# Cross-attention block in split f16: TensorE's program without a loop, maxima over the partitions by TensorE and VectorE, two weight loads later, causal mask added by VectorE

## The chip, the cores and the metric

The kernel runs on 1 core of one Trainium2 chip. A core has five engines that run programs of their own and meet at semaphores: TensorE (PE, with its weight loads as PEld), VectorE (DVE), ScalarE (ACT), GpSimd (POOL) and SyncE (SP), which here issues every DMA. The metric is the device time in microseconds (us) of one execution; lower is better.

## The reference

Eight batches of 1024 queries attend to 64 context rows of their own view, with 16 heads of 32 columns, and a feed-forward layer of 2048 follows:

```python
q = _layer_norm(query, ln1_g, ln1_b)
qh = (q @ wq + bq).reshape(Bq, Sq, H, hd)
kh = (context @ wk + bk).reshape(Bq, Sc, H, hd)
vh = (context @ wv + bv).reshape(Bq, Sc, H, hd)
scores = jnp.einsum('bqhd,bkhd->bhqk', qh, kh) * scale
allowed = pos_in_block[None, :] <= jnp.arange(Sq)[:, None]
scores = jnp.where(allowed[None, None, :, :], scores, NEG_INF)
probs = jax.nn.softmax(scores, axis=-1)
o = jnp.einsum('bhqk,bkhd->bqhd', probs, vh).reshape(Bq, Sq, Dm)
x = query + (o @ wo + bo)
h = _layer_norm(x, ln2_g, ln2_b)
return x + jax.nn.gelu(h @ w1 + b1, approximate=False) @ w2 + b2
```

Query is 8 x 1024 x 512, context 8 x 64 x 512, all f32. With 64 keys the causal mask touches only the first 64 queries of a batch, so only the first tile of 128 queries.

## The kernel before, in words

**Arithmetic.** Every f32 matrix product is made of three f16 products (`triple`, L1060: high x high, high x low, low x high). The f16 parts need a power-of-two scale for each operand, found at run time from the largest magnitude of each weight, bias and context matrix. Each partition's own maximum goes into a column of `maxima`; the maximum over the 128 partitions is needed on all of them in `gmax`. There are four such rounds: 0 (context, wk, wv, bk, bv), 1 (wq, first norm, query bias), 2 (wo, second norm, w1, its bias) and 3 (w2). Before, GpSimd does a round with `partition_all_reduce` in `reduce_maxima` (L478), at four places in its program.

**Stages.** A prologue transposes the context, finds scales, projects keys and values of all batches (`values`, in part inside the first slot) and takes the query tiles 0 to 3 through the first norm. Then come 17 slots. Slot c handles the attention of chunk c (512 queries, 4 tiles of 128; an even c starts a batch) and, woven between, the feed-forward of chunk c-1. Slots 0 and 16 have one half only. A slot has 19 groups; group g issues the first feed-forward product g (L1060 into ff1_ps), the attention steps that the tables `PLAN` or `PLAN_FIRST` (slot 0) give at position 2g, the second product g-3 (L1267), and the steps at position 2g+1. Each engine walks the same table and does its share of a step.

**Steps.** Q: query projection; S: scores of a tile on TensorE (L1184), row maximum (L985) and subtraction (L987) on VectorE; E: exponential on ScalarE; U: row sum and reciprocal on VectorE; then GpSimd divides (L540, `normalise`); Z, L: split into high and low f16 (ScalarE, VectorE), after which SP issues a DMA transpose of the probabilities (L419); V: values product (L1206), which waits for all four transposes; O: output projection, residual and norm statistics; H (slot 0) or G, D: second norm; W (slot 0): values product of the context. GpSimd also makes the reciprocal deviation of every norm (`rstd_of`, L483) in program order with its other work.

**Mask.** At tile 0 of an even slot two matmuls (L1178) first write the mask, `causal`, into the score bank with the identity `ident_bf`, and the score matmuls add to it.

**Loops.** In `slots` every engine writes slots 0 and 1 out, runs slots 2i+2 and 2i+3 in a hardware loop of 7 passes (GpSimd, ScalarE, VectorE and SP of 6, with the last two slots written out) and ends with slot 16.

**Loads.** SP's program is one ordered queue: context, wk, wv, wq, the first x tiles, wo, four pieces of w1, w2 pieces 2 and 3, then `move_values` (copies inside SBUF that wait for the values), then w2 pieces 0 and 1 (their place in SBUF is taken by early data until then), then slot 0's `move_probs`. ScalarE takes the magnitudes of w2 pieces 0 and 1 (L608) at position 20 and 21 of slot 0.

## Time and profile before

| | us |
|---|---|
| median of 3 runs | 1900.4 |
| range | 1899.72 to 1901.34 |
| the profiled execution, its own time | 1901.46 |
| the span in its trace | 1899.7 |

| engine | busy us | share |
|---|---|---|
| TensorE matmul | 1801.5 | 95% |
| VectorE | 1240.3 | 65% |
| ScalarE | 628.6 | 33% |
| GpSimd | 437.3 | 23% |

A trace row gives start, duration, engine, source line, operation, output and inputs, and in brackets how long the engine was idle before it and what ended that. "issue" is time in which the engine waited for nothing that the trace shows.

### The profile page before, as it was taken

To read this page: it belongs to the slowest core of one execution; us is meant where nothing else is said; L and a number is where in the kernel's file an instruction comes from. 1 tells how busy PE (TensorE), PEld (TensorE's weight loads), DVE (VectorE), ACT (ScalarE), POOL (GpSimd) and SP (SyncE) were. 2 spreads that over 40 slices of the span, in tenths; PEclk is the share of its full clock that TensorE was granted. 3 is DMA by queue.
4 is the path that set the end of the run, shared out by engine and by line. 5 is a ranking of instruction groups with operands and counts; after the bars stand their busy time and mean duration, and the time that the engine had idled before them with its cause. 6 is when DMAs were issued, how large, how long until landed. Compare 5 with 4: busy or idle time off the path is not lost.

```text
span 1899.7 us, 26840 instructions
## 1 busy us (share of the span) xinstructions
PE 1801.5 (95%) x10214; PEld 819.9 (43%) x10214; DVE 1240.3 (65%) x1905; ACT 628.6 (33%) x786; POOL 437.3 (23%) x380
## 2 busy tenths in 40 slices
PE   4737899999999999999999999999999999999999
PEld 2313344444444444444444444444444444444444
DVE  5757966757676675757676575767667576766632
ACT  3434523333242422324242232424233242424211
POOL 2431313122131313203141211313131121313200
PEclk9868999999999999999999999999999999999999
DMA  8051230413323141322314042231404123230300
GB/s 282 12 122 34 45 89 6 84 45 56 79 45 89 23 79 35 62 72 45 90 23 89 23 79 57 45 89 33 95 8 89 45 50 85 45 90 7 60 23 22
DMA packets 287751, 116.48 MB, mean 61 GB/s; under 512 B 262616, under 2 KB 264192, under 8 KB 287616
## 3 DMA queue, kind: packets, MB, share of 16 engines
q1 hardware_dynamic: 287616, 114.61, 27.5%
q8 instruction: 93, 1.52, 0.3%
q14 instruction: 42, 0.34, 0.1%
HBM read 31.22 MB, written 16.78 MB: 25 GB/s over the span
## 4 chain that ended last, share of the span: by engine, by line
PE 89%; DVE 5%; issue 2%; DMA 1%; ACT 1%; SPq 1%; POOL 1%; DVEq 0%; POOLq 0%; ACTq 0%
PE ff_ps L1060 34%; PE ff_ps L1267 33%; PE at_ps L1060 17%; PE at_ps L1184 2%; PE at_ps L1206 1%; DVE w_all L781 1%; DMA arena<-qT 1%; SPq L419 1%; DVE ssum L1003 0%; DMA arena<-in_L_xattn_wk 0%; DVE arena L781 0%; DVE xhat L770 0%; DVE stats L748 0%; DVE arena L987 0%; DVE smax L985 0%
## 5 line engine op out<-in xcount | busy, mean ns | idle before, releaser
L1060 PE MATMUL ff_ps<-arena,w_all 128*128 128x512 f16 x3072 | 703.8, 381 | 11.2 <-ACT arena L710 5.1
L1267 PE MATMUL ff_ps<-w_all,arena 128*128 128x512 f16 x3072 | 698.0, 379 | 0.8 <-DVE arena L781 0.8
L1060 PEld LDWEIGHTS ff_ps<-arena,w_all 128*128 128x128 f16 x3072 | 300.1, 98 | 384.1 <-issue 25.2
L1267 PEld LDWEIGHTS ff_ps<-w_all,arena 128*128 128x128 f16 x3072 | 294.3, 98 | 358.5 <-issue 6.4
L710 ACT ACTIVATE arena<-ff_ps,b1p,scales 128x512 f32<-128x512 f32 x256 | 198.7, 776 | 648.6 <-PE ff_ps L1060 648.3
L1033 DVE TENSOR_SCALAR arena<-arena,scales 128x512 f16<-128x512 f32 x256 | 140.9, 551 | 220.5 <-ACT arena L710 220.5
L781 DVE SCALAR_TENSOR_TENSOR arena<-arena,scales 128x512 f16<-128x512 f32 x256 | 240.1, 938 | 9.1
L483 POOL TENSOR_TENSOR rstd<-ve,minus_half 128x1 f32<-128x1 f32 x128 | 85.8, 670 | 545.8 <-DVE ve L753 537.8
L535 POOL TENSOR_TENSOR x_sb<-x_sb,bo_row 128x512 f32<-128x512 f32 x64 | 90.8, 1450 | 353.0 <-PE at_ps L1184 353.0
L648 ACT ACTIVATE norm_hl<-xhat 128x512 f16<-128x512 f32 x120 | 73.9, 628 | 290.6 <-DVE xhat L770 290.6
L540 POOL TENSOR_TENSOR arena<-arena,rsum 128x1024 f32<-128x1024 f32 x64 | 124.8, 1971 | 180.7 <-DVE rsum L1006 180.7
L1060 PE MATMUL at_ps<-wo_hi,act_T 128*128 128x512 f16 x512 | 156.0, 381 | 2.1 <-DVE act_T L781 2.1
L1060 PE MATMUL at_ps<-act_T,wq_hi 128*128 128x512 f16 x512 | 152.3, 379 | 0.0
L985 DVE TENSOR_REDUCE smax<-at_ps 128x16 f32<-128x1024 f32 x62 | 74.9, 1209 | 55.6 <-PE at_ps L1184 55.5
L979 DVE CAST qT<-arena 128x512 f16<-128x512 f32 x64 | 31.3, 489 | 114.6 <-ACT arena L652 114.6
L652 ACT ACTIVATE arena<-at_ps,bqp,scales 128x512 f32<-128x512 f32 x64 | 49.8, 778 | 150.1 <-PE at_ps L1060 150.1
L1060 PE MATMUL at_ps<-wo_lo,act_T 128*128 128x512 f16 x256 | 97.8, 382 | 0.0
L1060 PE MATMUL at_ps<-act_T,wq_lo 128*128 128x512 f16 x256 | 97.0, 379 | 0.0
L781 DVE SCALAR_TENSOR_TENSOR act_T<-at_ps,act_T 128x512 f16<-128x512 f32 x68 | 43.9, 686 | 72.0 <-ACT act_T L670 72.0
L777 DVE TENSOR_TENSOR norm_hl<-xhat,norm_hl 128x512 f16<-128x512 f32 x120 | 83.3, 694 | 5.1 <-ACT norm_hl L648 3.6
L546 POOL TENSOR_TENSOR arena<-arena,b_row 128x512 f32<-128x512 f32 x64 | 84.1, 1342 | 0.9 <-DVE xhat L770 0.9
L781 DVE SCALAR_TENSOR_TENSOR qT<-arena,qT 128x1024 f16<-128x1024 f32 x64 | 77.1, 1243 | 5.5 <-ACT qT L667 5.5
(131 smaller groups left out, 1320.1 us busy)
## 6 DMA issues: line engine op xcount, KB each, us to landing
x_sb<-in_x SPq DMA_DIRECT2D x64, 256.0 KB, 2.7
out_x<-arena SPq DMA_DIRECT2D x64, 256.0 KB, 2.1
w_all<-in_L_xattn_w SPq DMA_DIRECT2D x6, 1024.0 KB, 11.4
arena<-in_L_xattn_w SPq DMA_DIRECT2D x2, 1024.0 KB, 15.4
v_sb<-v_sb SPq DMA_DIRECT2D x6, 192.0 KB, 3.1
arena<-in_ctx SPq DMA_DIRECT2D x1, 1024.0 KB, 5.3
arena<-in_L_xattn_wk SPq DMA_DIRECT2D x1, 1024.0 KB, 7.9
arena<-in_L_xattn_wv SPq DMA_DIRECT2D x1, 1024.0 KB, 7.4
```

The source lines that it names most:

```text
L483: nc.gpsimd.tensor_tensor(rstd[:, n:n + 1], ve[:, n:n + 1], minus_half[:, :], ALU.pow).then_inc(ln_rstd, 1)
L535: nc.gpsimd.tensor_tensor(x_sb[:, t], x_sb[:, t], bo_row[:, :], ALU.add).then_inc(xb_set, 1)
L540: nc.gpsimd.tensor_tensor(pr, pr, rsum[:, t, :].unsqueeze(2).to_broadcast([P, HEADS, SC]), ALU.mult).then_inc(p_norm, 1)
L546: nc.gpsimd.tensor_tensor(x1[1 - par][:, t], x1[1 - par][:, t], b2_row[:, :], ALU.add).then_inc(x1b_set, 1)
L648: nc.scalar.activation(norm_hl[:, t, 0], xhat[:, t % 2], ACT.Copy).then_inc(n_hi, 1)
L710: nc.scalar.activation(gelu_full[g % 2], ff1_ps[:, g % 2, :], ACT.Gelu, bias=b1p[:, g:g + 1], scale=col(C1)).then_inc(g_full, 1)
L777: nc.vector.tensor_tensor(norm_hl[:, t, 1], xhat[:, t % 2], norm_hl[:, t, 0], ALU.subtract).then_inc(n_lo, 1)
L781: nc.vector.scalar_tensor_tensor(lo, src, factor, hi, ALU.mult, ALU.subtract).then_inc(done, 1)
L985: nc.vector.tensor_reduce(smax[:, t, :], scores, AX_X, ALU.max).then_inc(s_max, 1)
L1033: nc.vector.tensor_scalar(pair[:, 0, :], gelu_full[g % 2], col(SG), None, ALU.mult).then_inc(g_hi, 1)
L1060: last = nc.tensor.matmul(out_ap, s, m, start=(i == 0), stop=(i == n - 1))
L1267: last = nc.tensor.matmul(ff2_ps[:, t, :], pair[:, s, rows], m[:, j], start=(j == 0 and i == 0), stop=(j == NJ - 1 and i == 2))
```

## The change

- **Loop.** TensorE's 17 slots are a Python loop that writes all instructions out; the other engines keep theirs. Its waits compare with constants.
- **Maxima.** `reduce_maxima` on GpSimd is gone. For each round TensorE transposes the columns of `maxima` into PSUM, VectorE takes the maximum of each row and multiplies it onto a small diagonal, TensorE multiplies with a matrix of ones, which spreads it over the partitions, and VectorE copies that into `gmax`. Rounds 0 and 1 lie in the prologue, 2 and 3 at positions of slot 0 (`REDUCE_AT`). The scales of the feed-forward, which VectorE worked out at position 3, come at position 8.
- **Loads.** w2 pieces 0 and 1 are issued behind slot 0's transposes instead of ahead of them.
- **Mask.** The two matmuls are gone; VectorE adds `causal` while it moves the scores of tile 0 from PSUM into `probs`, and maximum and subtraction read `probs`.

```diff
-SCALES_AT = 3
+SCALES_AT = 8
+REDUCE_AT = {2: (4, 6), 3: (22, 24)}
...
             move_values(1, slice(2, BATCH))
-            for n in W2_ORDER[2:]:
-                load_w2(n)
...
                     for t in range(TT):
                         move_probs(c, t)
+                    if isinstance(c, int) and c == 0:
+                        for n in W2_ORDER[2:]:
+                            load_w2(n)
...
-            def reduce_maxima(n):
-                if n < len(ROUNDS) - 1:
-                    pool.wait_ge(max_ready[n], 1)
-                nc.gpsimd.partition_all_reduce(gmax[:, ROUNDS[n]], maxima[:, ROUNDS[n]], P,
-                                               bass.bass_isa.ReduceOp.max).then_inc(gmax_ready[n], 1)
...
+            def maximum_rows(n):
+                w = widths[n]
+                dve.wait_ge(rows_ps[n], 1)
+                link(nc.vector.reduce_max(row_max[0:w, n:n + 1], turned[n], AX_X))
+                nc.vector.tensor_scalar(on_diagonal[0:w, n, 0:w], ident[0:w, 0:w], row_max[0:w, n:n + 1], None,
+                                        ALU.mult).then_inc(diagonal_set[n], 1)
+            def maxima_everywhere(n):
+                dve.wait_ge(gmax_ps[n], 1)
+                link(nc.vector.tensor_copy(gmax[:, ROUNDS[n]], spread[n]))
...
+                        if batch is not None and t == 0:
+                            if isinstance(c, int) and c == 0:
+                                dve.wait_ge(const_set, 2)
+                            rows = probs[t].rearrange("p (e h k) -> p e h k", e=2, k=SC)
+                            nc.vector.tensor_tensor(rows, halves(c, t).rearrange("p e (h k) -> p e h k", k=SC),
+                                                    causal[:, :, :].unsqueeze(1).to_broadcast([P, 2, HEADS // 2, SC]),
+                                                    ALU.add).then_inc(masked, 1)
+                            dve.wait_ge(masked, batch + 1)
+                            scores = probs[t].rearrange("p (h k) -> p h k", k=SC)
...
+            def maximum_rows(n):
+                if n < len(ROUNDS) - 1:
+                    pe.wait_ge(max_ready[n], 1)
+                if n >= 2:
+                    pe.wait_ge(sums_ready, 1 if n == 2 else N2 + 1)
+                nc.tensor.transpose(turned[n], maxima[:, ROUNDS[n]], ident[:, :]).then_inc(rows_ps[n], 1)
+            def maxima_everywhere(n):
+                pe.wait_ge(diagonal_set[n], 1)
+                nc.tensor.matmul(spread[n], ones[0:widths[n], :], on_diagonal[0:widths[n], n, 0:widths[n]],
+                                 start=True, stop=True).then_inc(gmax_ps[n], 1)
...
-                        masked = batch is not None and t == 0
-                        if masked:
-                            for e in range(2):
-                                nc.tensor.matmul(halves(c, t)[:, e], ident_bf[:, :],
-                                                 causal[:, :, :].rearrange("p h k -> p (h k)"), start=True, stop=False)
...
-            slots(pe, slot)
+            for c in range(NCHUNK):
+                slot(c, c % 2, True, c > 0, None if c % 2 else c // 2)
+            slot(NCHUNK, 0, False, True, None)
```

GpSimd's program in the prologue, before (L478 with `gmax` is the reduction, the ISA rows around it set up the pool's configuration, L490 makes the low half of wv, L496 that of the keys, L483 the norm's factor):

```order
L478 ISA
L478 ISA gmax<-maxima 128x5 [waits max_ready0]
L490 ISA
L490 TENSOR_TENSOR w_all<-arena,w_all 128x512 [waits wv_scaled] x4
L478 ISA
L478 ISA gmax<-maxima 128x3 [waits max_ready1]
L496 ISA
L496 TENSOR_TENSOR kT_sb<-w_all,kT_sb 128x512 [waits kv_hi,const_dve]
L483 TENSOR_TENSOR rstd<-ve,minus_half 128x1 [waits ln_ve]
```

The same place now:

```order
L481 AFFINE_SELECT causal<-causal 128x512
L491 TENSOR_TENSOR w_all<-arena,w_all 128x512 [waits wv_scaled] x4
L496 TENSOR_TENSOR kT_sb<-w_all,kT_sb 128x512 [waits kv_hi,const_dve]
L486 TENSOR_TENSOR rstd<-ve,minus_half 128x1 [waits ln_ve]
L496 TENSOR_TENSOR kT_sb<-w_all,kT_sb 128x512 [waits kv_hi]
```

Both reductions and the three configuration rows are gone from between the elementwise instructions.

VectorE's program in slot 0, from the scores of tile 1 to those of tile 3, now (L1007 and L1009 are maximum and subtraction, L1025 and L1028 sum and reciprocal, L795 the copy into `gmax`, L916 to L927 the feed-forward's scales, of which eight rows are left out):

```order
L1007 TENSOR_REDUCE smax<-ff_ps 128x16 [waits s_ps]
L1009 TENSOR_TENSOR arena<-ff_ps,smax 128x1024 [waits s_max]
L1025 TENSOR_REDUCE ssum<-arena 128x16 [waits e_set]
L1028 RECIPROCAL rsum<-ssum 128x16 [waits s_sum]
L795 COPY gmax<-ff_ps 128x7 [waits gmax_ps2]
L1007 TENSOR_REDUCE smax<-at_ps 128x16 [waits s_ps,chain]
...
L916 TENSOR_REDUCE tmp<-gmax 128x1
L917 TENSOR_SCALAR tmp<-tmp 128x1 [waits chain]
...
L927 TENSOR_SCALAR scales<-power 128x1 [waits chain]
L1007 TENSOR_REDUCE smax<-ff_ps 128x16 [waits s_ps,scales_ready2]
```

Before, the same 13 scale rows stood ahead of the scores of tile 0; they have moved between those of tiles 2 and 3.

SP's program from the last copy of the values to the first x loads, before:

```order
L408 DMA v_sb<-v_sb 64x3x512
L392 DMA w_all<-in_L_xattn_w 128x4x512 x2
L419 DMA_TRANSPOSE arena<-qT 128x16x128 [waits z_lo] x4
L424 DMA x_sb<-in_x 128x512 [waits x1_set] x4
```

And now:

```order
L417 DMA v_sb<-v_sb 64x3x512
L425 DMA_TRANSPOSE arena<-qT 128x16x128 [waits z_lo] x4
L401 DMA w_all<-in_L_xattn_w 128x4x512 x2
L430 DMA x_sb<-in_x 128x512 [waits x1_set] x4
```

The two loads of w2 (1 MB each) have moved from ahead of the four transposes to behind them.

## Rows read from the trace of the kernel before

**Rows 1.** The page: busy time, TensorE's granted clock, an instruction queue (packets, MB, share).

```profile
PE 1801.5 (95%) x10214; PEld 819.9 (43%) x10214; DVE 1240.3 (65%) x1905; ACT 628.6 (33%) x786; POOL 437.3 (23%) x380
...
PEclk9868999999999999999999999999999999999999
...
q8 instruction: 93, 1.52, 0.3%
```

**Rows 2.** Busy time by window: window, length, busy per engine, clock, DMA; slots 2, 4, 15.

```profile
279.59:388.91 109.32, 109.32 (x628) 49.88 (x626) 73.95 (x113) 36.02 (x44) 27.57 (x24) 1.00 0.29 60
...
498.34:608.39 110.05, 109.63 (x627) 50.00 (x628) 73.34 (x112) 36.02 (x44) 27.54 (x24) 1.00 0.28 57
...
1704.44:1813.33 108.89, 108.89 (x626) 49.70 (x624) 68.02 (x93) 33.77 (x40) 27.78 (x20) 1.00 0.19 39
```

**Rows 3.** TensorE's waits: total us, times, longest.

```profile
PE at_ps L1206 <- DMA arena<-qT: 39.2, 2, 33.6
PE at_ps L1103 <- DVE xhat L770: 11.5, 3, 9.7
...
PE ff_ps L1060 <- issue: 4.7, 10, 0.7
```

**Rows 4.** GpSimd's timeline, 0 to 160 us: the reductions and what follows them.

```profile
36.17 0.38 POOL L478 PARTITION_ALL_REDUCE gmax<-maxima  x1 [6.10 <-issue]
43.60 1.14 POOL L496 TENSOR_TENSOR kT_sb<-w_all,kT_sb 128x512 f16<-128x512 f32 x1 [7.05 <-issue]
...
86.19 1.25 POOL L503 TENSOR_TENSOR w_all<-w_all 128x512 f32<-128x512 f32 x1 [7.66 <-issue]
...
141.31 1.21 POOL L483 TENSOR_TENSOR rstd<-ve,minus_half 128x1 f32<-128x1 f32 x2 [8.00 <-issue]
```

**Rows 5.** VectorE's timeline, 0 to 160 us.

```profile
15.28 0.17 DVE L841 TENSOR_SCALAR bound<-gmax 128x3 f32<-128x3 f32 x1 [0.57 <-POOL gmax L478]
...
99.47 1.78 DVE L781 SCALAR_TENSOR_TENSOR qT<-arena,qT 128x1024 f16<-128x1024 f32 x1
...
103.47 2.28 DVE L781 SCALAR_TENSOR_TENSOR qT<-arena,qT 128x1024 f16<-128x1024 f32 x1
...
141.94 0.55 DVE L770 TENSOR_SCALAR xhat<-arena,mv,rstd 128x512 f32<-128x512 f32 x1 [5.00 <-POOL rstd L483]
```

**Rows 6.** SP's timeline in slot 0.

```profile
99.80 1.41 SPq L392 DMA_DIRECT2D w_all<-in_L_xattn_w  x2
101.35 16.84 SPq L419 DMA_TRANSPOSE arena<-qT  x4
```

**Rows 7.** Line 419 alone, 92 to 135 us: issue to landing; ScalarE's wait for it.

```profile
DMA to landing us min/median/max: 4.3/4.4/9.9
111.34 1.06 ACT L667 ACTIVATE qT<-arena 128x1024 f16<-128x1024 f32 x1 [10.27 <-DMA arena<-qT]
```

**Rows 8.** TensorE's timeline, prologue and slot 0.

```profile
9.88 0.33 PE L1074 MATMUL at_ps<-ident,vec_rows 40*128 40x40 f32 x1
...
59.49 5.34 PE L1083 MATMUL ff_ps<-w_all,cols 128*32 128x512 f32 x32 [2.10 <-DVE wq_lo L781]
...
120.73 1.48 PE L1206 MATMUL at_ps<-arena 64*32 64x512 f16 x24 [33.61 <-DMA arena<-qT]
...
152.07 6.91 PE L1060 MATMUL ff_ps<-arena,w_all 128*128 128x512 f16 x24 [1.50 <-DVE arena L781]
```

**Rows 9.** VectorE's timeline in slot 8: tile 0's scores, the low half of a gelu.

```profile
964.79 1.22 DVE L985 TENSOR_REDUCE smax<-at_ps 128x16 f32<-128x1024 f32 x1 [1.84 <-PE at_ps L1184]
966.05 1.22 DVE L987 TENSOR_TENSOR arena<-at_ps,smax 128x1024 f32<-128x1024 f32 x1
...
967.75 1.64 DVE L781 SCALAR_TENSOR_TENSOR arena<-arena,scales 128x512 f16<-128x512 f32 x1
970.86 1.23 DVE L985 TENSOR_REDUCE smax<-at_ps 128x16 f32<-128x1024 f32 x1 [1.48 <-PE at_ps L1184]
```

**Rows 10.** TensorE's timeline in slot 8: tile 1's score matmuls.

```profile
969.97 0.84 PE L1184 MATMUL at_ps<-arena,qT 64*128 64x128 f16 x24
```

More of the change, by code:

```diff
@@ L211, in cross_attention_block @@
         gmax = sb("gmax", [P, M2 + N2], F32)
+        row_max = sb("row_max", [P, 4], F32)
+        on_diagonal = sb("on_diagonal", [P, 4, 8], F32)
+        ones = sb("ones", [P, P], F32)
         LC, LK, LV, LBK, LBV, LQ, LBQ, L1, LO, LBG, L2 = range(11)
@@ L237, in cross_attention_block @@
         at_ps = ctx.enter_context(nc.psum_tensor("at_ps", [P, 2, CHUNK], F32))
+        widths = [r.stop - r.start for r in ROUNDS]
+        turned = [(at_ps[:, 0, :] if n < 2 else ff2_ps[:, 3, :])[0:w, P:2 * P] for n, w in enumerate(widths)]
+        spread = [(at_ps[:, 0, :] if n < 2 else ff2_ps[:, 3, :])[:, 2 * P:2 * P + w] for n, w in enumerate(widths)]
         bias_bank = (at_ps[:, 1, :], ff1_ps[:, 0, :])
@@ L256, in cross_attention_block @@
             "bias_rows_ps", "bias_rows_set", "biases_ps"))
-        max_ready, gmax_ready, scales_ready = ([sem(f"{n}{i}") for i in range(4)] for n in (
-            "max_ready", "gmax_ready", "scales_ready"))
+        max_ready, scales_ready, rows_ps, diagonal_set, gmax_ps = ([sem(f"{n}{i}") for i in range(4)] for n in (
+            "max_ready", "scales_ready", "rows_ps", "diagonal_set", "gmax_ps"))
         sums_ready = sem("sums_ready")
@@ L737, in _ @@
             nc.vector.memset(minus_half[:, :], -0.5).then_inc(chain, 1)
-            links[0] += 2
-            dve.wait_ge(chain, 2)
+            nc.vector.memset(ones[:, :], 1.0).then_inc(chain, 1)
+            links[0] += 3
+            dve.wait_ge(chain, 3)
             for h in range(GH):
@@ L837, in powers @@
                 link(nc.vector.reciprocal(r(first, last), a(first, last)))
-            dve.wait_ge(gmax_ready[0], 1)
+            maximum_rows(0)
+            maxima_everywhere(0)
             link(nc.vector.tensor_scalar(bounds(LC, LV), gm(MC, MV), TINY, None, ALU.max))
@@ L870, in query_scales @@
             def query_scales():
-                dve.wait_ge(gmax_ready[1], 1)
+                maximum_rows(1)
+                maxima_everywhere(1)
                 link(nc.vector.tensor_scalar(gm(MQ, MG1), gm(MQ, MG1), TINY, None, ALU.max))
@@ L955, in aside @@
                         feed_forward_bias()
+                    for n, (rows_at, spread_at) in REDUCE_AT.items():
+                        if position == rows_at:
+                            maximum_rows(n)
+                        if position == spread_at:
+                            maxima_everywhere(n)
                     if position == SCALES_AT:
@@ L1096, in _ @@
             pe.wait_ge(cols_set, 1)
+            maximum_rows(0)
+            maxima_everywhere(0)
             pe.wait_ge(w_loaded[W_Q], 16)
@@ L1123, in _ @@
                                              for k in range(KT)]).then_inc(kv_ps, 1)
+                if m == 0:
+                    maximum_rows(1)
+                elif m == 1:
+                    maxima_everywhere(1)
             for t in range(2):
@@ L1185, in step @@
                                                             kblk[half, a, g].rearrange("p h k -> p (h k)"),
-                                                            start=(i == 0 and not masked),
-                                                            stop=(i == 2 and (g == KT - 1 or not masked)))
+                                                            start=(i == 0), stop=(i == 2))
                         last.then_inc(s_ps, 1)
@@ L1255, in slot @@
                             step(kind, t)
+                    if isinstance(c, int) and c == 0:
+                        for n, (rows_at, spread_at) in REDUCE_AT.items():
+                            if 2 * g == rows_at:
+                                maximum_rows(n)
+                            if 2 * g == spread_at:
+                                maxima_everywhere(n)
                     if ff and g >= LAG:
```

15 lines of the change are left out of this document (2 added, 13 removed).

## The prediction

> **What bounds the kernel now.** The page comes first. TensorE is busy for 95% of the span, VectorE for 65%, and the granted clock is in its top tenth in every slice but three of the first four [rows 1]. So there are two kernels in one: a steady part that TensorE fills, and a beginning where it waits. The view of windows, cut where each slot's first feed-forward product starts, shows the steady part. Slot 15 takes 108.89 us and TensorE is busy for all of it; slot 2 takes 109.32; slot 4, the first after a jump back, 110.05 [rows 2]. The reader should see that nothing another engine does can shorten such a slot: only fewer matmuls, or fewer stalls inside TensorE's own program. TensorE's list of waits then shows where the rest is: 39.2 us for the transposed probabilities, 33.6 of it once, in slot 0, and 11.5 us for normalised tiles, 9.7 of it once, in the prologue; ten stalls of at most 0.7 us have no releaser at all [rows 3]. All but these ten lie before 280 us.
>
> **The change, part by part.** Times below are those of the trace of before; "early" is how much sooner the same event comes.
>
> *The loop.* From 279.59 to 1813.33 us there are 14 slots in 1533.74 us [rows 2]. At slot 15's 108.89 they would take 1524.46. The difference is 9.28. Slot 2 is straight behind slot 1 without a jump and starts a batch, so its excess, 109.32 - 108.89 = 0.43, is the two mask matmuls; seven such slots make 3.0. The remaining 6.3 us come with six jumps back, 1.04 each, seen as the stalls without a releaser [rows 3]. Written out, TensorE's program has no jump, so I take all 6.3 away. The bounds: 0 if the stalls stay where they are, 6.3 if they go. The straight runs, slot 1 into 2 and slot 15 into 16, show none, which is why I take the upper end.
>
> *The mask.* The two matmuls go: 3.0 us in slots 2 to 14, and 0.5 in slot 0 that the chain below absorbs. VectorE gets one more instruction of 128x1024 in eight slots. The trace has no such add; the nearest is the subtraction with one operand in PSUM, 1.22 us [rows 9]. Its upper bound is 2.28, the same size with both operands in SBUF while GpSimd works [rows 5]. What hides it: TensorE needs the bank back for tile 1's scores at 969.97 [rows 10]. VectorE starts tile 0 at 964.79 [rows 9], and add, maximum and subtraction at 1.22 each end at 968.5; with the subtraction at 2.28, 969.6. Both are ahead of 969.97, so TensorE pays nothing. Queued behind it on VectorE are a gelu pair (0.5 + 1.64) and tile 1's maximum, which had 1.48 us of idle time before it [rows 9]; the 1.2 us fill that. The cover is 1.5 us and no more: see the rivals. One rule bears on it. In rows, an operation on two SBUF operands took 2.28 instead of some 1.2 [rows 5]. The Trainium skill, "SBUF — State Buffer", section "Who interferes with whom", says that a VectorE instruction with two SBUF inputs and a GpSimd instruction that reads SBUF exclude each other, so that the later waits for the whole of the other. By that rule the subtraction, which now reads SBUF twice, is the one that suffers, and the sum stays the same, since 969.6 is its worst case.
>
> *Maxima, round 0.* GpSimd answered in 0.57 us [rows 5]. The new way is two small f32 matmuls (0.33 each [rows 8]), and three small VectorE instructions of 0.17 [rows 5] with four handoffs: some 1.7 us with the latency of each. The start is 1.1 late. The bounds are 0.8 and 2 late. The Trainium skill, "VectorE: DVE Perf Modes", section "Rules for kernel authors", sends reductions over the partitions to GpSimd; this round agrees, by 1.1 us; what the rule would make of all four is among the rivals.
>
> *Round 1.* The reduction itself shows 0.38 us, but GpSimd is idle without cause for 6.10 before it and 7.05 after it [rows 4]; it is as if code was being changed for it and back. All the while the keys' low half and the norm's factor wait, and so TensorE, 9.7 us [rows 3]. Without it, I walk the chain anew: first key product 25.3 to 30.4, VectorE's statistics end at 31.8, the round is spread at 33.7 behind the second key product, the third and fourth products run to 38.9, their evictions and GpSimd's small work keep up, and the first transposes start at 38.9 instead of 46.8. That is 7.9 early. The values product behind it no longer follows an idle stretch, so it takes 2.6 instead of 4.4 us, and the wq conversions end correspondingly earlier. The bias product at 59.49 [rows 8] then starts at 48.4, 11.1 early; the lower bound is the 7.9.
>
> *Round 2 and tile chain in slot 0.* GpSimd's next instruction came at 86.19 after 7.66 idle us [rows 4], 3.3 after its input; that goes. VectorE gains the mask add (1.2) and three small operations (0.6). The 13 scale operations (2.7) only move, from ahead of tile 0 to ahead of tile 3, and are still in its serial chain. Net 0.3 more: VectorE's first low half of probabilities (99.47 [rows 5]) comes 11.4 early. Bounds: 8 and 13.
>
> *The two loads.* SP issues 2 MB [rows 6] right ahead of the first transpose. That transpose landed after 9.9 us, where the others took 4.3 to 4.4, and ScalarE waited 10.27 us for it, until 111.34 [rows 7]; VectorE had been ready with the second low half at 105.7 (103.47 + 2.28 [rows 5]). Behind the transposes, the loads disturb none. The first transpose then no longer holds the second; the chain is second low half, 94.3, plus 4.4 to land, ScalarE and VectorE 2.3, last transpose 4.4: values product at 105.7 instead of 120.73 [rows 8], 15.0 early. So this part is worth 3.6. Its cost: the loads land at about 112, and ScalarE needs them at about 114. x loads queue behind them and are wanted later still. Bounds for the part: 0 and 6.
>
> *Round 3.* GpSimd again: 8.00 us before the norm's factors [rows 4], and VectorE stuck for 5.00 of them [rows 5] while TensorE still had output projections to do. Anew: factors in 0.7 us each, second-norm transposes directly behind the projections, their last low half 3.6 sooner than the one that released 152.07 [rows 8], counting 0.6 for the new VectorE work. Bounds: 2 and 5.
>
> The sum: 11.4 + 3.6 + 3.6 early at the end of slot 0, 18.6; slot 1 keeps its length, since its waits are its own; then 6.3 + 3.0. Together **27.9 us**. The profiled execution took 1901.46 for a span of 1899.7; the median of the runs is 1900.4. Taken off the median: **1872.5**.
>
> **Rivals.** *The beginning gives less.* The chain binds elsewhere, at the clock or a conversion: bounds 7.9 instead of 11.1, and 0 and 2 for loads and round 3. Then the gain is 7.9 + 0.3 + 0 + 2 + 9.3 = 19.5: 1881. For it: the chain has three engines in turn and I worked it out. Against: GpSimd's idle stretches are plain, and nothing else is due then. *It gives more:* clock better, ends at 13, 6 and 5 with 9.3: 33, so 1867. *The mask binds.* If all three of VectorE's operations take 2.28, they end at 971.6 + handoff, 1.8 us after TensorE wants the bank; seven slots: 12.6 lost, 1885. Against it: maximum and subtraction next to GpSimd's work stood at 1.22 [rows 9]. *Slower: straight code stalls.* The page counts 93 packets on the larger instruction queue, some five a slot [rows 1]. If a written-out program stalls at each as it did at most at a jump, 0.7 us [rows 3], it loses 65 us: the 21.6 gained without the loop's 6.3 turn into 43.5 lost, 1943.9. It decides from 21.6 / 93 = 0.23 us per packet. Against it: slots 2 and 15 are straight code too, and show none [rows 2]. *The change does nothing for GpSimd*, if it is idle there for another reason than the reduction: the four rounds then each cost 1.1 more, as round 0 does, and 9.3 + 3.6 - 4.4 = 8.5 are gained, 1891.9. Against: the idle time stands around the reductions only [rows 4]. That is how it would come out by the rule of the Trainium skill on reductions over the partitions, on the page named above.
>
> **How the numbers follow.** Forecast 1872.5 with its own spread of 1868 to 1877: 0.6. Less at the beginning: 0.15. More: 0.1. Mask binds: 0.06. GpSimd idle anyway: 0.03. Straight code stalls: 0.04. The last 0.02 is for no change by something unseen. The range takes the first three and the mask's price: 1862 to 1885. Faster by over 0.2% (about what a measurement of this kernel can tell from no change) 0.94, within 0.2% 0.02, slower 0.04.
>
> **What would show it.** In the trace of after: no stall without releaser on TensorE behind 280 us, and every full slot at 108.9; the wait of 33.6 us down to about 17; GpSimd without idle stretches of 6 to 8 us that have no releaser; all transposes landing in 4.3 to 4.5 us; tile 1's score matmuls not waiting for VectorE in even slots; the first feed-forward product at about 133.5 instead of 152.07. It is wrong if an even slot takes over 109.2 us, or if TensorE's first values product comes after 110.

## The result, and the profile after

The changed kernel takes **1872.95 us** (median of 4 runs, 1871.0 to 1874.73) against 1900.74 for the kernel before in the same session. The ratio is 0.9854, with a 95% interval of 0.9837 to 0.9871: 27.8 us, or 1.5%, faster. The forecast was 1872.5. The profiled execution took 1874.73 for a span of 1872.9, so it stands 1.8 above its median, where that of before stood 0.7 above.

The page of after, the parts that answer to [rows 1]: busy time, TensorE's granted clock, the larger instruction queue (packets, MB, share).

```profile
PE 1796.0 (96%) x10210; PEld 819.0 (44%) x10210; DVE 1261.5 (67%) x1925; ACT 629.4 (34%) x786; POOL 443.7 (24%) x376
...
PEclk9869999999999999999999999999999999999999
...
q8 instruction: 80, 1.31, 0.3%
```

The windows of after for slots 2, 4 and 15, as in [rows 2] (window, length, busy time of each engine, clock, DMA share, GB/s):

```profile
262.17:371.06 108.89, 108.89 (x626) 49.70 (x624) 76.25 (x114) 36.13 (x44) 28.57 (x24) 1.00 0.29 60
479.95:588.84 108.89, 108.89 (x625) 49.72 (x624) 76.27 (x114) 36.13 (x44) 28.58 (x24) 1.00 0.27 59
1677.74:1786.63 108.89, 108.89 (x625) 49.72 (x624) 68.09 (x93) 33.77 (x40) 27.64 (x20) 1.00 0.20 39
```

Every slot now takes the 108.89 us that only slot 15 took. From the start of slot 2 to the end are 1872.9 - 262.17 = 1610.7 us, where before there were 1899.7 - 279.59 = 1620.1: **9.4 us** gained in the steady part. Slot 2 starts 279.59 - 262.17 = **17.4 us** earlier. These two are the whole difference of the spans, 26.8.

TensorE's list of waits in after, against [rows 3] (total us, times, longest):

```profile
PE at_ps L1239 <- DMA arena<-qT: 36.0, 2, 30.5
PE ff_ps L1091 <- DMA arena<-in_ctx: 6.6, 1, 6.6
PE at_ps L1127 <- ACT arena L610: 6.1, 1, 6.1
PE at_ps L1104 <- DVE maxima L798: 4.6, 1, 4.6
PE ff_ps L1082 <- ACT arena L706: 3.6, 1, 3.6
...
PE ff_ps L1108 <- DVE on_diagonal L790: 1.4, 1, 1.4
```

The ten stalls without a releaser are gone, and of the wait of 9.7 us for a normalised tile 1.5 us are left. The 4.6 and 1.4 us (L1104, L1108) are the new rounds' own waits, in the prologue. The long wait for the transposed probabilities has shrunk by 3.1 us only: it both begins and ends earlier.

TensorE's timeline in after: the bias product, the first values product, and the first feed-forward product of slot 1, which answer to [rows 8] (start, length, operation, in brackets idle time and its releaser).

```profile
49.04 5.26 PE L1118 MATMUL ff_ps<-w_all,cols 128*32 128x512 f32 x32 [2.10 <-DVE wq_lo L777]
...
108.15 1.48 PE L1239 MATMUL at_ps<-arena 64*32 64x512 f16 x24 [30.54 <-DMA arena<-qT]
...
135.31 8.19 PE L1082 MATMUL ff_ps<-arena,w_all 128*128 128x512 f16 x24 [1.57 <-DVE arena L777]
```

They come 10.5, 12.6 and 16.8 us earlier than in [rows 8]. The beginning varies between executions: in two more traces of the same kernel the values product starts at 106.62 and 105.38, so 14.1 and 15.3 earlier (c1_after and c3_after below, in this order wherever "the other two traces" are named).

### The profile page after: what moved, and what is told of

Same layout as the page of the kernel before. It is cut to its first block, busy times and chain, and to the rows that moved or that the text cites. A ratio compares the mean times of both kernels' runs of the same rounds, so it can differ in the third digit from the quotient of the medians.

```text
span 1872.9 us, 26516 instructions
## 1 busy us (share of the span) xinstructions
PE 1796.0 (96%) x10210; PEld 819.0 (44%) x10210; DVE 1261.5 (67%) x1925; ACT 629.4 (34%) x786; POOL 443.7 (24%) x376
## 4 chain that ended last, share of the span: by engine, by line
PE 91%; DVE 6%; DMA 1%; ACT 1%; issue 1%; SPq 0%; POOL 0%; DVEq 0%; ACTq 0%
PE ff_ps L1082 35%; PE ff_ps L1306 34%; PE at_ps L1082 17%; PE at_ps L1219 2%; PE at_ps L1239 1%; DVE w_all L777 1%; DMA arena<-qT 0%; DVE qT L777 0%; DMA arena<-in_L_xattn_wv 0%; DVE arena L777 0%; DVE ssum L1025 0%; DVE arena L1009 0%; DVE smax L1007 0%; DVE wo_lo L777 0%; DVE xhat L766 0%
## 5 line engine op out<-in xcount | busy, mean ns | idle before, releaser
L1055 DVE TENSOR_SCALAR arena<-arena,scales 128x512 f16<-128x512 f32 x256 | 150.1, 586 | 212.7 <-ACT arena L706 212.6
L535 POOL TENSOR_TENSOR x_sb<-x_sb,bo_row 128x512 f32<-128x512 f32 x64 | 95.5, 1523 | 349.1 <-PE at_ps L1219 349.1
L546 POOL TENSOR_TENSOR arena<-arena,b_row 128x512 f32<-128x512 f32 x64 | 87.2, 1392 | 1.3 <-DVE xhat L766 1.3
L1007 DVE TENSOR_REDUCE smax<-at_ps 128x16 f32<-128x1024 f32 x54 | 65.0, 1204 | 27.1 <-PE at_ps L1219 27.1
L1040 DVE SCALAR_TENSOR_TENSOR arena<-at_ps,scales,x_sb 128x512 f32<-128x512 f32 x64 | 47.9, 749 | 49.3 <-PE at_ps L1082 49.2
```

What stands on the lines that cost most here:

```text
L535: nc.gpsimd.tensor_tensor(x_sb[:, t], x_sb[:, t], bo_row[:, :], ALU.add).then_inc(xb_set, 1)
L546: nc.gpsimd.tensor_tensor(x1[1 - par][:, t], x1[1 - par][:, t], b2_row[:, :], ALU.add).then_inc(x1b_set, 1)
L1007: nc.vector.tensor_reduce(smax[:, t, :], scores, AX_X, ALU.max).then_inc(s_max, 1)
L1055: nc.vector.tensor_scalar(pair[:, 0, :], gelu_full[g % 2], col(SG), None, ALU.mult).then_inc(g_hi, 1)
```

## The experiments

Each kernel is the changed one with one edit, save where it is said. Times are medians of 4 to 10 runs, and differences are taken against the changed kernel, which was run again beside them:

| kernel | edit | us | against after | ratio to before (95%) |
|---|---|---|---|---|
| c1_after | none | 1872.26 | | 0.9842 (0.9829 to 0.9854) |
| c3_after | none | 1872.74 | | 0.9847 (0.9832 to 0.9862) |
| e1_loop | TensorE's loop back | 1898.46 | +26.2 | 0.9978 (0.9967 to 0.9989) |
| e5_maxima_only | kernel before with the new maxima | 1910.46 | +37.7 | 1.0043 (1.003 to 1.0056) |
| e2_mask_pe | mask by TensorE | 1873.14 | +0.9 | 0.9848 (0.9836 to 0.9861) |
| e3_loads_first | the two loads ahead of the transposes | 1872.95 | +0.7 | 0.9843 (0.983 to 0.9856) |
| e4_reduce_r1 | a GpSimd reduction in round 1's place | 1887.28 | +14.8 | 0.9927 (0.9914 to 0.9939) |
| e7_reduce_idle | the same where GpSimd is idle | 1872.01 | -0.5 | 0.985 (0.9836 to 0.9864) |
| e8_reduce_r3 | the same in round 3's place | 1876.32 | +3.8 | 0.9877 (0.9862 to 0.9891) |
| e10_add_x2 | mask added twice | 1872.38 | -0.4 | 0.9844 (0.9829 to 0.9858) |
| e6_add_x3 | mask added three times | 1894.30 | +22 | 0.996 (0.9948 to 0.9973) |
| e9_scales_later | scales behind the second low half | 1868.86 | -3.9 | 0.983 (0.9815 to 0.9845) |

The kernels e4, e7, e8 and e6 ran without the control beside them; they are set against 1872.5, the mean of its two medians. In their session the kernel before took 1899.92, where it took 1902.25 and 1901.85 in the other two; set against it they would be some 2 us slower than the table says, and their differences are uncertain by that much. So for them the traces decide.

### The changed kernel again

> The changed kernel again, as the mark for the three kernels beside it. Both theories: 27 to 28 us below the kernel before, about 1872.9.

> The changed kernel again, as the mark for the three kernels beside it: 27 to 28 us below the kernel before.

1872.26 (1870.89 to 1873.34) and 1872.74 (1872.26 to 1873.82). The result holds, and differences under about 1 us say nothing here.

### The loop alone

```diff
-            for c in range(NCHUNK):
-                slot(c, c % 2, True, c > 0, None if c % 2 else c // 2)
-            slot(NCHUNK, 0, False, True, None)
+            slots(pe, slot)
...
                             pe.wait_ge(v_lo, 4 * c + 2)
+                        pe.sem_inc(values_begun, 1)
```

> The changed kernel with TensorE's program in its loop again (and the one semaphore increment ahead of the values product that the loop form needs), all else as changed. Theory: the stalls without a releaser come back at the jumps back, 6.3 us in all, so the time is that of the changed kernel plus 6.3, about 1879.2, and the larger instruction queue counts about 93 packets again instead of 80. Rival: straight code costs something of its own that the changed kernel pays in the gaps between matmuls, and the loop is within 2 us of the changed kernel.

Measured: 1898.46 (1893.57 to 1905.28), 26.2 us slower, not 6.3. Both expectations missed by far. TensorE's list of waits in this kernel has the stalls without a releaser again, and longer ones:

```profile
PE ff_ps L1083 <- issue: 17.9, 12, 2.9
```

[Rows 3] have 4.7 us, 0.7 at most. TensorE's timeline at the jump back into slot 4 shows where they lie. This is the kernel with the loop:

```profile
479.16 1.02 PE L1083 MATMUL ff_ps<-arena,w_all 128*128 128x512 f16 x4 [0.43 <-issue]
482.78 12.57 PE L1083 MATMUL ff_ps<-arena,w_all 128*128 128x512 f16 x44 [2.60 <-issue]
```

The same place in the kernel before:

```profile
498.34 3.18 PE L1060 MATMUL ff_ps<-arena,w_all 128*128 128x512 f16 x14 [0.54 <-issue]
501.94 7.50 PE L1060 MATMUL ff_ps<-arena,w_all 128*128 128x512 f16 x34 [0.42 <-issue]
...
717.71 10.55 PE L1060 MATMUL ff_ps<-arena,w_all 128*128 128x512 f16 x48 [0.43 <-issue]
```

In both, a jump is followed by one stall of 0.3 to 0.7 us at once and by a second one some matmuls later: 14 matmuls in the kernel before, 4 in this one. From the loop's first matmul to the end of the second stall it is 3.60 us before (498.34 to 501.94) and 3.62 us here (479.16 to 482.78). So it looks as if something that takes some 3.6 us arrives then; 14 matmuls hide 3.0 to 3.2 us of it, and 4 hide 0.9 to 1.0.

The 44 matmuls behind the stall then take 12.57 us, where 44 at the 0.216 us of a matmul in a full slot are 9.5. The window over them shows why:

```profile
482.78:495.30 12.52, 12.52 (x45) 5.14 (x46) 3.71 (x6) 2.33 (x3) 0.00 (x0) 0.76 0.03 10
```

The granted clock is 0.76 there, between its two levels of 1.2 and 2.4 GHz (0.5 and 1.00), after 3 us of stalls; over the like stretches behind the other five jumps it is 0.76 to 0.88. In the kernel before it stayed at 1.00 behind its shorter ones. The five full passes behind a jump take 222.5 to 224.2 us in this trace, against 2 x 108.89 = 217.8: 5.5 us a jump, of which 3.0 are stalls and most of the rest the clock. The sixth takes 221.6, and all together are some 31 us. The profiled execution was the slowest of ten and also began slot 2 some 2 us later than the control's; the median over all runs is 26.2.

### The maxima alone, put into the kernel before

The edit takes the loop, the mask matmuls and the early loads of the kernel before, and the maxima of the new one. Only the loads are shown here:

```diff
             move_values(1, slice(2, BATCH))
+            for n in W2_ORDER[2:]:
+                load_w2(n)
...
                         move_probs(c, t)
-                    if isinstance(c, int) and c == 0:
-                        for n in W2_ORDER[2:]:
-                            load_w2(n)
```

> The kernel before with the maxima on TensorE and VectorE (and the scales at position 8) as the one part of the change; loop, mask matmuls and loads as before. Theory: the parts add up: 27.8 less 6.3, 3.0 and 3.7, so 14.8 us below the kernel before. Rival: the parts overlap, and the maxima alone are worth 17 or more, or 12 or less.

Measured: 1910.46 (1904.62 to 1914.73): **slower** than the kernel before, by 8.6 us, where 14.8 us less was expected. The rival's "12 or less" covers it by its words, but nobody expected a loss. Its beginning does what it should: slot 2 starts at 259.21, 20.4 us earlier than in [rows 2]. The loop then gives back more. TensorE's list of waits in this kernel, and its timeline at the first jump:

```profile
PE ff_ps L1075 <- issue: 22.4, 12, 3.2
```

```profile
478.21 0.59 PE L1075 MATMUL ff_ps<-arena,w_all 128*128 128x512 f16 x2 [0.80 <-issue]
481.70 12.65 PE L1075 MATMUL ff_ps<-arena,w_all 128*128 128x512 f16 x46 [2.89 <-issue]
```

Here 2 matmuls stand between the stalls, the first of which is longer too (0.7 to 0.9 us), and from the loop's first matmul to the end of the second stall it is 3.49 us (478.21 to 481.70): the same arrival, hidden by 2 matmuls instead of 14.

The counts of matmuls explain 14, 4 and 2. First the page of this kernel:

```profile
PE 1814.2 (95%) x10226; PEld 823.2 (43%) x10226; DVE 1243.2 (65%) x1918; ACT 628.7 (33%) x786; POOL 436.3 (23%) x376
```

It has 10226 matmuls, the kernel before 10214 [rows 1]. The 12 more are the four rounds, one transpose and two matmul records of the spread each, and all stand ahead of the loop: 14 - 12 = 2. The kernel with the loop alone also lacks the mask, of which two matmuls stood ahead of the loop, in slot 0: 12 - 2 = 10 more ahead of it, and 14 - 10 = 4. By these counts the second stall belongs to a fixed place in TensorE's program, counted from its start, and the loop's first instruction has moved towards it. The page's instruction queue supports this reading: 93 packets in all three kernels with a loop, 80 written out, 13 fewer for six jumps. The Trainium skill, "Runtime: NRT & Kernel Launch", section "Instruction fetch mechanics", says that an engine's program is fetched in order, in blocks, and that a taken branch out of the blocks held has to wait for a fetch. The traces agree, and add the size: 3.3 to 3.9 us from the first matmul to the second stall's end in the three kernels, at nearly every jump. At two jumps, those to 717.71 and 1594.94, the kernel before shows no second stall, as fits an arrival just behind its 14 matmuls. What was not run is a loop kernel with filler ahead of the loop, which would prove the place.

### The mask

```diff
-                            nc.vector.tensor_tensor(rows, halves(c, t)..., causal..., ALU.add).then_inc(masked, 1)
...
+                        if masked:
+                            for e in range(2):
+                                nc.tensor.matmul(halves(c, t)[:, e], ident_bf[:, :], causal..., start=True, stop=False)
```

> The changed kernel with the causal mask put in by TensorE's two matmuls again and without VectorE's add. Theory: 0.43 us in each of seven steady slots, 3.0 us slower than the changed kernel, less up to 1.2 us that VectorE's chain in slot 0 gets back: plus 1.8 to 3.0. Rival: VectorE's add costs TensorE's next step something, so that giving it back to TensorE changes nothing or gains: minus 1 to plus 1.

Measured: 1873.14 (1873.12 to 1874.24), 0.9 us slower, at the edge of what can be told, half of the least that was expected and inside the rival's range. Its reason, a cost to TensorE's next step, isn't seen: the tile behind the new add never waits. In the traces both halves of the trade are plain. The first full slot takes 366.74 - 257.42 = 109.32 us by TensorE's timeline, so 0.43 more, as before; seven times that is 3.0. But VectorE's serial chain in slot 0 has one operation of 1.2 us less: from the start of the bias product to the first values product it is 56.53 us here (48.57 to 105.10), against 57.65 and 57.47 in the two traces of the control; the maxima put into the kernel before, also without the add, have 56.62. So the new mask gains 3.0 where TensorE is the limit and loses about 1 us in slot 0, where VectorE is. That leaves 2; the 0.9 measured differs from it by no more than the scatter, and the spans differ by 1.5 and 0.5 us from those of the two controls.

The cover of the new operation was measured with more of the same:

```diff
-                            nc.vector.tensor_tensor(rows, ..., ALU.add).then_inc(masked, 1)
+                            for i in range(times_added):     # 1 in slot 0, then 2 (e10) or 3 (e6)
+                                nc.vector.tensor_tensor(rows, ..., ALU.add).then_inc(masked, 1)
```

The operation is repeated with the same result.

> The changed kernel with VectorE's mask add done twice in the seven even slots behind slot 0. Theory: one more add of 1.25 us fits into the 1.4 us of cover: plus 0 to 1. Rival: GpSimd's work on the shared port makes the longer chain overlap with more of its instructions, and each even slot takes 0.5 us more: plus 3.5 or more.

> The changed kernel with VectorE's mask add done three times over in the seven even slots behind slot 0 (each writes the same values; slot 0 has it once). Theory: in the trace of the changed kernel the subtraction ends at 945.95 and TensorE wants the bank at 947.39, so the cover left is 1.4 us; two more adds of 1.25 are 2.5, and TensorE waits 1.1 us per slot: plus 7 to 9 in all. Rival: the delay runs on through the transposes into the values product, or is taken up by VectorE's other idle time: plus 15 or more, or plus 0 to 1.

Two additions cost nothing that can be told (1872.38; in the trace TensorE waits in one of the seven slots, 0.89 us), three cost 22 us (1894.3, 1889.3 to 1895.45) where 7 to 9 were expected. In after, VectorE's timeline in slot 8 reads:

```profile
942.21 1.22 DVE L1002 TENSOR_TENSOR arena<-at_ps,causal 128x1024 f32<-128x1024 f32 x1 [1.40 <-PE at_ps L1219]
943.47 1.22 DVE L1007 TENSOR_REDUCE smax<-arena 128x16 f32<-128x1024 f32 x1
944.73 1.22 DVE L1009 TENSOR_TENSOR arena<-arena,smax 128x1024 f32<-128x1024 f32 x1
```

The subtraction ends at 945.95, and TensorE starts the scores of tile 1 at 947.39, with no wait. With three additions it looks like this on VectorE in slot 4:

```profile
504.22 3.74 DVE L1004 TENSOR_TENSOR arena<-at_ps,causal 128x1024 f32<-128x1024 f32 x3 [1.41 <-PE at_ps L1221]
507.99 1.22 DVE L1009 TENSOR_REDUCE smax<-arena 128x16 f32<-128x1024 f32 x1
509.25 2.36 DVE L1011 TENSOR_TENSOR arena<-arena,smax 128x1024 f32<-128x1024 f32 x1
```

and on TensorE:

```profile
511.67 0.84 PE L1221 MATMUL at_ps<-arena,qT 64*128 64x128 f16 x24 [2.21 <-DVE arena L1011]
512.44 4.45 PE L1308 MATMUL ff_ps<-w_all,arena 128*128 128x512 f16 x12
```

Three things add up. The two additions cost 2.5 us, of which 1.4 are covered. The subtraction, now later, starts together with the first operation of another group on GpSimd (L546), and one of the two is held up. In six slots it is the subtraction, with 2.36 us (2.27 once) instead of 1.22. In slot 2 the two start as close together, but GpSimd's is the longer one, so TensorE waits only 1.07. VectorE and GpSimd in slot 2, then GpSimd in slot 4:

```profile
290.34 1.22 DVE L1011 TENSOR_TENSOR arena<-arena,smax 128x1024 f32<-128x1024 f32 x1
290.36 2.33 POOL L546 TENSOR_TENSOR arena<-arena,b_row 128x512 f32<-128x512 f32 x1
...
509.27 1.26 POOL L546 TENSOR_TENSOR arena<-arena,b_row 128x512 f32<-128x512 f32 x1
```

And behind a wait of 2.21 us the next 12 matmuls take 4.45 us instead of 2.76 in four slots; in slot 12, behind the same wait, they take 2.76, so a wait of this length doesn't always cost clock. The seven waits sum to 14.2 us, the slower matmuls to 8.4 (1.69 in four slots, 0.60 + 1.02 in slot 14, none in two), together the 22.6 by which the span is longer. The rival's 15 or more fits in size only: TensorE has no other wait in these slots, so nothing runs on into the values product.

In after the subtraction starts 0.08 us ahead of one of GpSimd's L535 operations in six of the seven slots and stays at 1.22. It is then GpSimd's operation that is longer, 2.26 instead of 1.27. In slot 14 the subtraction starts 0.01 us behind it and takes 2.33; it ends at 1600.38, and TensorE starts the scores of tile 1 at 1600.71, still without a wait. GpSimd's timeline in after (slot 8), and with three additions (slot 4), where the subtraction comes later:

```profile
942.36 6.12 POOL L535 TENSOR_TENSOR x_sb<-x_sb,bo_row 128x512 f32<-128x512 f32 x4 [7.33 <-PE at_ps L1219]
```

```profile
504.36 4.95 POOL L535 TENSOR_TENSOR x_sb<-x_sb,bo_row 128x512 f32<-128x512 f32 x4 [7.33 <-PE at_ps L1221]
```

The rule of "SBUF — State Buffer", section "Who interferes with whom", of the Trainium skill has the later of the two wait for the whole of the other; 1.17 us more on GpSimd in one slot and 1.14 more on VectorE in the other agree with it. Where the recorded starts lie 0.02 us apart, as in slots 2 and 4 above, either was the one that waited.

### The two loads

```diff
             move_values(1, slice(2, BATCH))
+            for n in W2_ORDER[2:]:
+                load_w2(n)
...
-                    if isinstance(c, int) and c == 0:
-                        for n in W2_ORDER[2:]:
-                            load_w2(n)
```

> The changed kernel with w2 pieces 0 and 1 issued ahead of slot 0's transposes again. Theory: they share the queue with the first transpose, which lands after some 10 us instead of 4.4, and the values product of slot 0 starts 3.6 us later: plus 3.6. Rival: since GpSimd no longer delays that stretch, SP has issued the loads (from 87 us) some 5 us before the first transpose is due at 92.5, so that a good part of their 7 us of transfer is over and the transpose is late by 2 us or less: plus 0 to 2.

Measured: 1872.95 (1871.44 to 1873.31), 0.7 us, no difference that can be told; the rival held. SP's timeline in this kernel:

```profile
84.46 1.41 SPq L401 DMA_DIRECT2D w_all<-in_L_xattn_w  x2
89.92 13.16 SPq L427 DMA_TRANSPOSE arena<-qT  x4
```

In [rows 6] the loads were issued 1.55 us ahead of the first transpose, since the copies of the values ahead of them waited for a late GpSimd. Now they go out 5.46 us ahead, and the transposes land in 4.2 to 5.0 us (median 4.3) in spite of them. From the first transpose's issue to TensorE's values product it is 15.65 us here (89.92 to 105.57) and 15.70 in the control (90.92 to 106.62).

### The reduction on GpSimd, in three places

A reduction whose result nobody reads is added to GpSimd's program:

```diff
+            pool.wait_ge(max_ready[1], 1)
+            nc.gpsimd.partition_all_reduce(unused_max[:, :], maxima[:, ROUNDS[1]], P, bass.bass_isa.ReduceOp.max)
```

> The changed kernel with one reduction over the partitions put back on GpSimd at the place of round 1, between the low halves of wv and of the keys; its output is not used, so nobody waits for its answer. Theory: what round 1 cost was the change of GpSimd's code, 6 us before it and 7 after, in which the keys' low half and the norm's factors wait: plus 7 to 10.5. Rival: what it cost was VectorE's wait for the answer; with the answer unused, plus 0 to 1.

> The changed kernel with the same unused reduction on GpSimd at 56 us, where GpSimd is idle for 15.6 us. Theory: the change of code there and back takes 13.2 us, which fits into the gap: plus 0 to 0.5, with two idle stretches of 6 to 8 us in GpSimd's timeline around it. Rival: a reduction costs time wherever it stands (by what it does to memory or the queues): plus 3 or more.

> The changed kernel with the same unused reduction at the place of round 3, ahead of the second norm's factors. Theory: about 7 to 8 us without a releaser after it, in which the factors wait; since TensorE has output projections to do for part of it, plus 3.5 to 4.5. Rival: GpSimd has time for it before the factors are due, plus 0 to 1.

GpSimd's timeline with it in round 1's place:

```profile
36.80 0.38 POOL L494 PARTITION_ALL_REDUCE unused_max<-maxima  x1 [6.14 <-issue]
44.72 1.14 POOL L499 TENSOR_TENSOR kT_sb<-w_all,kT_sb 128x512 f16<-128x512 f32 x1 [7.54 <-issue]
```

Both idle stretches of [rows 4] are back, around an instruction of 0.38 us, and with them 14.8 us (1887.28, 1884.78 to 1888.0), more than the 7 to 10.5 expected; the rival of 0 to 1 fell. The bias product starts at 61.29 against 48.97 in the control, 12.3 later, and the first values product at 120.46, where the kernel before had 120.73 [rows 8]. Part of it is the clock: the bias product takes 5.34 us at a granted clock of 0.68 here, as in the kernel before, and 3.64 at 1.00 in both controls. So this one round was nearly the whole gain of the prologue.

Where GpSimd has nothing to do, the same instruction:

```profile
60.44 0.38 POOL L559 PARTITION_ALL_REDUCE unused_max<-maxima  x1 [5.61 <-issue]
68.79 1.29 POOL L504 TENSOR_TENSOR w_all<-w_all 128x512 f32<-128x512 f32 x1 [7.97 <-ACT w_all L675]
```

costs nothing (1872.01, 1871.15 to 1872.26): GpSimd's next input is what ends its second idle stretch, and from the bias product to the first values product it is 57.45 us, as in the controls. In round 3's place it costs 3.8 us (1876.32, 1875.56 to 1878.02), as expected; in the traces the first feed-forward product follows the first values product by 31.4 us instead of 26.5, so 4.9. GpSimd's norm factor starts late again:

```profile
117.21 0.39 POOL L568 PARTITION_ALL_REDUCE unused_max<-maxima  x1 [18.44 <-ACT arena L608]
125.05 1.21 POOL L487 TENSOR_TENSOR rstd<-ve,minus_half 128x1 f32<-128x1 f32 x2 [7.46 <-issue]
```

What the idle stretches are the rows don't say; their place and length fit a change of code, there and back. The Trainium skill, "GPSIMD Engine Reference", section "2.1 Instruction dispatch", says that the first call of a freshly loaded routine pays some 6 us that no instruction shows. The stretches ahead of the reduction, 6.14 and 5.61 us, agree. The one behind it, 7.5 us, is known from these runs and [rows 4] alone.

### The scales later

```diff
-SCALES_AT = 8
+SCALES_AT = 13
...
+                if position == 15:
+                    return list(range(CONV_Q, CONV_O))
```

VectorE's 13 scale operations move behind the first two low halves, and the four conversions of wo, which need them, to position 15.

> A further step: the changed kernel with the feed-forward's scales at position 13 instead of 8 (behind the second low half of the probabilities) and the four conversions of wo all at position 15, behind the last low half, instead of one each at positions 12 to 15. Theory: the 4.0 us of scales and the 2.3 us of the first wo conversion leave VectorE's chain to the second transpose and go under the transposes' landing: minus 5 to 6.5 against the changed kernel. Rival: GpSimd's division or ScalarE's high halves come last there instead, minus 0 to 2, or the wo conversions are late for the output projection, plus 1 or more.

Measured: **1868.86** (1868.68 to 1871.35), 3.9 us faster than the changed kernel: the fastest version found. In the traces 2.2 us of it are seen: from the bias product to the first values product it is 55.29 us (47.79 to 103.08) against 57.47 in the control beside it (47.91 to 105.38). The other 1.7 us lie in slot 1, whose length differs by as much between traces of one kernel (125.7 and 128.0 in the two controls). It is less than the 5 to 6.5 expected, and VectorE's timeline shows one reason:

```profile
89.16 0.22 DVE L923 SCALAR_TENSOR_TENSOR bound<-bound,gmax 128x1 f32<-128x1 f32 x1
89.42 1.20 DVE L845 TENSOR_SCALAR power<-bound 128x3 int32<-128x3 int32 x1
...
90.86 0.97 DVE L840 TENSOR_SCALAR scales<-inverse 128x2 f32<-128x2 f32 x1
91.86 1.19 DVE L840 TENSOR_SCALAR gs<-cols,scales 128x4 f32<-128x4 f32 x1
```

The 13 operations, 2.7 us by themselves, take 5.5 (88.17 to 93.67) beside GpSimd's work, and ScalarE waits 9.70 us for them with the next high halves. So they have moved within the chain and not out of it.

## Why the prediction came out, point by point

The number was right to half a microsecond, and its two halves nearly: 9.4 us in the steady part against 9.3, 17.4 at the end of slot 1 against 18.6 (20.6 and 19.5 in the other two traces). For the beginning that is in part luck. The sum overrated one term by 1.9 us (round 2 below) and left out another: the bias product takes 5.34 us at a granted clock of 0.68 in the kernel before and 3.64 at 1.00 in eleven of the twelve traces without a reduction in round 1. Only the profiled execution of after has 5.26, and there the beginning falls short. The account of single terms is less good than the number.

- **The loop, 6.3.** Right as a difference between these two kernels: the stalls of [rows 3] are gone and no others came. The rival of stalling straight code fell. What the prediction lacked is that the price of the loop isn't its own. It took 1.04 us a jump as given; beside the new maxima it is about 4.4 (26.2 / 6). The step that would have failed is the silent one that the parts can be priced one by one. Undone singly, loop and round 1 alone come to 26.2 + 14.8 = 41 us of a change that is worth 27.8.
- **The mask, 3.0.** Right in the full slots, 108.89 each, and the cover of 1.5 us was 1.4 and decides where it was said to. Its cost in slot 0, named there as 1.2 in VectorE's chain, takes back about a third. The rival of the binding mask fell: its 1.8 us of lateness needed all three operations at 2.28. Add and maximum took 1.22, and the subtraction reached 2.33 in one slot of seven, where it ended 0.33 us ahead of TensorE, as the sum's worst case had it.
- **Round 0, 1.1 late.** Mis-sized by 0.3. The value came from setting 1.7 us for the new way against GpSimd's 0.57; in this trace it takes 1.96, from the end of the last maximum at 15.32 to the first use at 17.28, so it is 1.4 late. The scales come 2.0 late (18.37 against 16.38), since one weight also landed 0.6 later in that execution. That is at the upper bound given. VectorE's timeline in after, against [rows 5]:

```profile
15.87 0.28 DVE L789 TENSOR_REDUCE row_max<-at_ps 5x1 f32<-5x128 f32 x1 [0.56 <-PE at_ps L1104]
16.18 0.22 DVE L790 TENSOR_SCALAR on_diagonal<-ident,row_max 5x5 f32<-5x5 f32 x1
17.08 0.17 DVE L795 COPY gmax<-at_ps 128x5 f32<-128x5 f32 x1 [0.68 <-PE at_ps L1108]
17.28 0.17 DVE L850 TENSOR_SCALAR bound<-gmax 128x3 f32<-128x3 f32 x1
```

- **Round 1, bias product 11.1 early.** 10.5 (49.04; 10.5 and 11.6 in the other two traces). The walk along the chain was right: 11.1 with round 0's 1.1 in it is 12.2 for the round, and the experiment that puts the reduction back gives 12.3. That the product itself would be shorter by 1.7 at a higher clock wasn't in the sum.
- **Round 2, first low half 11.4 early.** 8.9 early in the profiled execution (90.58 instead of 99.47), 10.4 and 11.7 in the two other traces (89.04 and 87.82): about 1 too much on the mean. The step itself is further off, since the shorter bias product hides it in those two. From the start of the bias product to the low half it is 39.98 us before and 41.54 in after, with bias products of about the same length; it is 40.07 and 39.91 in the other two, with 1.7 us less of bias product. So the stretch lost 1.6 to 1.8 us where a gain of 0.3 was forecast. The sum doesn't follow from its own terms either: 3.3 gained on GpSimd against 1.2 and 0.6 makes 1.5, not 0.3. In the traces VectorE's idle time of 3.62 us ahead of the first row sum is gone, and the mask add takes 1.2 as said. But the prediction counted the three small operations as 0.6 and the moved scale operations as the same 2.7 as before; they take 1.3 and 4.0, two of them being longer beside GpSimd, and short waits make the rest. VectorE's timeline in after:

```profile
72.11 0.92 DVE L790 TENSOR_SCALAR on_diagonal<-ident,row_max 7x7 f32<-7x7 f32 x1
...
82.34 1.52 DVE L921 SCALAR_TENSOR_TENSOR bound<-bound,gmax 128x1 f32<-128x1 f32 x1
```

  Before, the latter took 0.16 with GpSimd idle. TensorE's timeline in c1_after, for the bias product at the higher clock:

```profile
48.97 3.64 PE L1118 MATMUL ff_ps<-w_all,cols 128*32 128x512 f32 x32 [2.10 <-DVE wq_lo L777]
```

  The move from position 3 to 8 put the scales beside GpSimd's division and into the chain that ends last, so its cover was gone, and the last experiment gives back 2.2 us of the chain.
- **The loads, 3.6.** Right in size by the traces (12.6 - 8.9 = 3.7, and 3.7 in the other two), wrong in cause. The transposes land in 4.2 to 4.4 us, as foretold, but they would also do so with the loads where they were, since an earlier GpSimd had already parted the two. In this kernel the 3.6 belong to the maxima, and the order of the loads is worth nothing that can be told (0.7). Whether the move alone would bring them in the kernel before wasn't run.
- **Round 3, 3.6.** 16.8 - 12.6 = 4.2 by the profiled execution, 4.8 by the other two, 3.8 by the experiment's median and 4.9 by its trace: within the bounds, and the term was too small.
- **The signs named.** All transposes at 4.3 us, no stall behind 280 us, no idle stretch of 6 to 8 us without a releaser on GpSimd (so the rival that it would be idle anyway fell), no wait in even slots and a feed-forward start at about 133.5 (135.31, and 133.14 and 131.88 in the other traces) were seen. One was wrong: the wait of 33.6 us was to fall to about 17 and stands at 30.5. The prediction moved the wait's end and forgot that its beginning, TensorE's last work ahead of it, moves by the same prologue. Before it began at 87.1, after at 77.6.

## What to carry to other kernels

Price a hardware loop by the place at which it starts in its engine's program: a dozen matmuls more ahead of it cost up to 5.8 us at each jump here (225.1 us a pass against 219.3), and a change that gains 20 us in a beginning can come out slower through its loop. Parts of a change that share a chain or a program can't be summed from runs that undo one each; put the interesting one alone into the old kernel as well. And before a small operation is moved to where it seems free, look at what GpSimd does there and which chain ends last.

## What the runs showed of the hardware

- Behind a jump back TensorE stalls 0.3 to 0.9 us at once, and again until 3.3 to 3.9 us from the loop's first matmul; the second stall is 0 to 0.7, 2.3 to 2.9 or 2.8 to 3.2 us with 14, 4 or 2 matmuls ahead of it.
- Gaps of 2.3 to 2.9 us in TensorE's work (the loop alone) were followed by a granted clock of 0.76 to 0.88 over the next 11 to 12.5 us, and one of 2.2 us by 12 matmuls in 4.45 instead of 2.76 us in four slots, but by 2.76 in another; gaps of up to 1.07 us left it at 1.00.
- A partition reduction of 0.38 us on GpSimd came with 5.6 to 6.1 us of idle time ahead of it and 7.0 to 8.0 behind it; one cost 14.8 us of the whole on the critical chain and nothing in a pause.
- When VectorE's subtraction with two operands in SBUF (1.22 us) and a GpSimd operation of 1.27 us started within 0.1 us of each other, exactly one of the two took about 1.1 us more.
- Tiny VectorE operations (0.16 to 0.23 us) took 0.92 to 1.52 us beside GpSimd's elementwise work, but only some of them.
